# Order of the windowed attention's jobs: one half of the heads through all parts first, then the other

## The reference, cut to what matters

```python
q = (xp @ Wq + bq).reshape(B, Lp, H, D).transpose(0, 2, 1, 3)       # H = 16 heads, D = 16
k = (xp @ Wk + bk).reshape(B, Lp, G, D).transpose(0, 2, 1, 3)       # G = 2 groups
v = (xp @ Wv + bv).reshape(B, Lp, G, D).transpose(0, 2, 1, 3)
# windows of 32 tokens, one every 16 tokens
qg = qw.reshape(B, R, G, num_windows, W, D)
scores = jnp.einsum('brgnqd,bgnkd->brgnqk', qg, kw) * scale
attn = jax.nn.softmax(scores, axis=-1)
og = jnp.einsum('brgnqk,bgnkd->brgnqd', attn, vw)
o = og.reshape(B, H, num_windows, W, D)
o = o.transpose(0, 2, 3, 1, 4).reshape(B, num_windows * W, H * D)
o = o[:, :L, :]
return o @ Wo + bo
```

## Time and profile before

| what | value |
|---|---|
| median of three runs | 1166.67 us (1164.44 to 1168.65) |
| the profiled execution | 1169.2 us, span 1167.4 us |
| TensorE (PE) busy | 1115.8 us, 96% |
| VectorE (DVE) / ACT / POOL busy | 64% / 45% / 21% |
| mean granted clock of TensorE | 0.971 |
| windowed attention's jobs | about 939 to 1019 us of the span |

### The profile page before, as it was taken

One profiled execution on the slowest core, in us unless ns is written; L12 is line 12 of the kernel. 1 busy time (PEld: TensorE's weight loads), 2 busy tenths in 40 slices (PEclk: granted clock), 3 DMA queues, 4 the chain that ended last, 5 costly groups with the idle time before them and its releaser, 6 DMA issues. The chain is left out here.

```text
span 1167.4 us, 20269 instructions
## 1 busy us (share of the span) xinstructions
PE 1115.8 (96%) x7188; PEld 959.3 (82%) x7188; DVE 743.5 (64%) x1583; ACT 525.2 (45%) x976; POOL 247.1 (21%) x283
## 2 busy tenths in 40 slices
PE   8999999999999999999999998889998779899997
PEld 7898988988989899899889997755555568778897
DVE  6665665665756756747657577745554866686656
ACT  6675344344344443443443554535551356544322
POOL 1112111111111111111111102123333636323211
PEclk9999999999999999999999999799998958999999
DMA  4001000001001001001000003733333324000001
GB/s 155 10 1 37 10 1 36 9 0 36 9 0 36 9 0 38 7 0 45 0 0 1 1 2 134 224 86 103 99 101 97 89 56 146 1 1 1 19 19 37
DMA packets 28001, 48.28 MB, mean 41 GB/s; under 512 B 4802, under 2 KB 18082, under 8 KB 26786
## 3 DMA queue, kind: packets, MB, share of 16 engines
q1 hardware_dynamic: 24002, 37.62, 9.9%
q0 software_dynamic: 3456, 9.44, 3.1%
q10 hardware_dynamic: 480, 0.40, 0.1%
HBM read 35.65 MB, written 9.44 MB: 39 GB/s over the span
## 5 line engine op out<-in xcount | busy, mean ns | idle before, releaser
L823 POOL TENSOR_TENSOR linear_out_row<-linear_out_row,lin_sq 128x512 f32<-128x512 f32 x62 | 88.4, 1426 | 566.8 <-ACT lin_sq L703 564.0
L43 PE MATMUL lin_bank<-keep_xT_hi,lin_w_hi 128*128 128x512 f32 x382 | 153.3, 401 | 0.0
L778 DVE TENSOR_TENSOR lin_st<-lin_bank,lin_mask 128x512 f32<-128x512 f32 x64 | 44.3, 692 | 170.1 <-PE lin_bank L587 170.1
L44 PE MATMUL lin_bank<-keep_xT_lo,lin_w_hi 128*128 128x512 f32 x382 | 150.7, 395 | 0.0
L45 PE MATMUL lin_bank<-keep_xT_hi,lin_w_lo 128*128 128x512 f32 x382 | 150.7, 394 | 0.0
L699 ACT ACTIVATE lin_o<-lin_bank 128x512 f32<-128x512 f32 x64 | 38.3, 598 | 185.2 <-PE lin_bank L618 185.2
L614 PE MATMUL lin_bank<-lin_st,lin_v 128*128 128x128 f32 x512 | 94.0, 275 | 0.0
L618 PE MATMUL lin_bank<-lin_qd,lin_state 128*128 128x128 f32 x448 | 87.2, 276 | 0.0
L45 PEld LDWEIGHTS lin_bank<-keep_xT_hi,lin_w_lo 128*128 128x128 f32 x382 | 71.9, 188 | 17.0
L44 PEld LDWEIGHTS lin_bank<-keep_xT_lo,lin_w_hi 128*128 128x128 f32 x382 | 72.0, 188 | 14.3
L43 PEld LDWEIGHTS lin_bank<-keep_xT_hi,lin_w_hi 128*128 128x128 f32 x382 | 71.9, 188 | 14.2
(11 more groups left out here) (417 smaller groups left out, 2837.5 us busy)
## 6 DMA issues: line engine op xcount, KB each, us to landing
lin_raw<-in_wp SPq DMA_DIRECT2D x7, 1024.0 KB, 4.8
experts_up_expert_up<-in_wgu SPq DMA_DIRECT2D x16, 352.0 KB, 7.3
sorted_y<-shared_loaded SPq DMA_DIRECT2D x40, 128.0 KB
lin_raw_out<-in_wop SPq DMA_DIRECT2D x8, 256.0 KB, 2.6
tokens_x<-linear_out_row SPq DMA_DIRECT2D x4, 512.0 KB, 8.3
linear_out_row<-in_ffn_up SPq DMA_DIRECT2D x2, 1024.0 KB, 5.7
tail_q<-tail_qT SPq DMA_DIRECT2D x28, 64.0 KB, 2.0
keep_x<-in_x SPq DMA_DIRECT2D x3, 512.0 KB, 7.4
```

What stands on the lines that cost most here:

```text
L43: nc.tensor.matmul(out, lh, rh, start=first, stop=False, skip_group_check=skip)
L44: nc.tensor.matmul(out, lh, rl, start=False, stop=False, skip_group_check=skip)
L778: dve.tensor_tensor(C4(st[:, a, :]), C4(bank[2 + a][:]), mask[:, a:a + 1, :].broadcast_to([P, TPS, P]), ALU.mult).then_inc(st_sb, 1)
L823: pool.tensor_tensor(part, part, sq[:, a, :], ALU.add).then_inc(squares_sb, 1)
```

## The change

Line 2391 now lists, for each sequence, all four parts of the first half of the heads and then all four of the second. With it, ACT's arrangement of the second half's part 0 for the first sequence, which stood ahead of the loop, is now done in step 2, ahead of part 1. Nothing else in the text changes; the output products are bound to jobs of the second half, and their steps follow the list.

```diff
-        JOBS = [(b, rr, mq) for b in range(BATCH) for mq in range(4) for rr in range(RR)]
+        JOBS = [(b, rr, mq) for b in range(BATCH) for rr in range(RR) for mq in range(4)]
...
                 values(0)
                 arrange(0, 0)
-                arrange(1, 0)
                 for i in range(NJ + 4):
...
                     if i == 2:
+                        arrange(1, 0)
                         arrange(1, 1)
```

## The result

The changed kernel takes 1185.97 us (median of 6 runs, 1181.35 to 1193.61), the kernel before beside it 1167.66 us (6 runs). The ratio is 1.0167, 95% interval 1.0146 to 1.0187: 18.3 us slower. Forecast were 1180.4 us and +13.7; the direction held, the size was short by a quarter, and the median lies above the 1176 to 1184 given to the forecast itself. The profiled execution (1193.61 us) is the slowest of the six, so its rows show more of the loss than the median has. The feed-forward is no part of it: from the first row behind the barrier to the end of the span are 1167.4 - 1019.59 = 147.8 us before and 1191.8 - 1043.99 = 147.8 us after.

What follows compares the result with a forecast made beforehand. TensorE was taken as the bound, busy 96% of the span, with holes in its clock. Start 0, middle +5.6, end +5.4 and end clock +2.7 sum to +13.7 on 1166.67: 1180.4 us, own range 1176 to 1184, whole range 1171 to 1186.

Steps and rivals of the forecast that it cites:

- Start, 0: First jobs of the stage: two edits of about 2 us each cancel; 0, bounds -2.5 and +2.1 us.
- Steps 8 to 10 at half clock: Middle: without wide products the fallen clock isn't raised; three steps of 4.47 us plus output product 3.65, from 975.1 to 992.2.
- 3 x 4.39 + 2.52 = 15.69: Middle, from the start of step 11 to step 15: full-clock steps, three with an output product, one without; 15.69 us.
- Added waits in steps 11 to 14: Middle: POOL's wait for VectorE and power instruction cost POOL some 2 us; 0 while covered, 2 us if not.
- The end, +5.4: From job 15's scores to the last add: four chained output products behind the last value product, 22.4 us against 17.0.
- its clock, +2.7: End of the stage: the clock falls, slowing one output product by 1.8 us and half the second by 0.9; bounds 0, +3.6.
- The middle's +5.6: Start of step 15 moves from 1002.30 to 1007.9 us if the clock falls in the middle; +0.1 if it never falls.
- The narrow work doesn't raise the clock: Steps 8 to 10: scores, transposes and value products leave a fallen clock at 0.50 until a wide product runs.
- Holds it only when dense: Middle: narrow work keeps an already granted full clock only if TensorE has little idle time; no size of its own.

Runs made afterwards that it cites:

- experiment 5: Kernel with only the second sequence in the new order, plus three idle products in each of two TensorE holes at the end: 1171.65 us.
- experiment 3: Changed kernel with idle products in step 2, four 256 columns wide or eight 128 wide, one execution each: 1187.88 and 1190.06 us.

## Why the prediction was right in direction and short in size

- *Start, 0.* Right: the two edits cancel. Jobs 0 to 8 were forecast to take 35.9 us (939.23 to 975.1) and took 38.1; the clock rose at 965 instead of 958.4. With the same start other kernels took 35.6 to 43.7 us, the clock rising 19 to 36 us behind job 0's scores. So this part varies more with the execution than with the order.
- *Steps 8 to 10 at half clock.* Right in the profiled execution. From job 8's scores to the end of output product 0 took 17.46 us, forecast 992.2 - 975.1 = 17.1. In the profile of the whole change with banks the clock held there, so which of the two happens changes from execution to execution.
- *"From there to the start of step 15 are three steps with an output product and one without: 3 x 4.39 + 2.52 = 15.69."* This is the step that failed. It took 1017.17 - 995.61 = 21.56 us. Three waits for the add make 3.6 of the missing 5.9; product 1, caught by another fall of the clock, makes 3.63 - 1.94 = 1.7; the last 0.5 is spread, step 11's scores being partly at half clock. I saw the one bank and its wait, and priced it at the end. In the middle I took the step from rows in which output products stand two steps apart, where the add has time. "Added waits in steps 11 to 14" looked at POOL alone, and that part was right: POOL's wait moved nothing.
- *The end, +5.4, and its clock, +2.7.* Right: 22.1 us to the last add at full clock in experiment 5, where the sum says 22.4 (before 17.0), and 4.8 + 2.8 us over before by the medians. In the profile after, two whole products were caught at half clock instead of one and a half.
- *The middle's +5.6* was meant as the clock alone. Counted over before, the banks took 4.3 us off the first sequence's 10.7 and the idle products another 6.0, and the end has 7.6. The 4.3 are about what the forecast lacks (13.7 against 18.3). How much of the 6.0 is the order's is open, since the idle products of step 6 help the kernel before as well.
- *"The narrow work doesn't raise the clock"* held in every profile where it was low in steps 8 to 10, but the word narrow was wrong (experiment 3), and the wide projections of the start didn't always raise it either. "Holds it only when dense" was not tested by itself, and a hole is not the whole of it. Behind the hole of 1.3 us in front of job 8's scores the clock fell in three profiles, and it held in the fourth that has this hole (the whole change with banks). And most falls around step 7 came with no hole over 0.3 us, 0.5 to 1.6 us behind the small turns of the values in step 6: in nine of the eleven profiles without idle products there, before and after alike. By the Trainium skill, "TensorE: Matmul & The Clock Gate", "Why this matters for your kernels", unbroken work should have raised it; 13.8 us of it in after did not, though a fifth to a quarter of it was transposes, which the prediction names as the exception.
- *Open.* Why the whole change with banks and idle products is 5 us above what I expected from its parts. In both profiles the clock fell in step 8, behind the hole of 1.3 us in front of job 8's scores. That this is all is argued, not shown, since no profile of those kernels held the clock up. And against the kernel before with its holes filled (fewer of them than here), the order with banks still costs some 12 us (5.6 over before against 7.1 under it); by the profiles, 31.2 against 23.5 us in the middle and 19.9 against 17.3 in the end.

## What to carry to other kernels

When a reordering bunches work that shares a buffer, take its price from the consumer's own order of instructions, not from rows in which it was spread: here the add stood behind a wait for scores, and a free engine couldn't run it. Look at what an order leaves to TensorE between two waits, since a low clock stretches all of it (a job's work from 2.52 to 4.65 us here); filling the holes took 7 us off, while the new order cost 18. And what is bunched behind the last value of a chain lies bare in front of a barrier.

## What was not expected of the hardware

Idle products made the kernel before faster: some 20 matmuls that compute nothing, in holes from 924 to 962 us, took 7 us off the median (1167.29 to 1160.20). And executions of one program differ with the clock: ten runs of one kernel took from 1166.97 us at a mean granted clock of 0.974 to 1180.75 us at 0.962, while the feed-forward behind the stage took 147.8 or 147.9 us in every profile.
